# The attention output's transpositions moved from VectorE's 32x32 blocks to TensorE, with quotients out of PSUM

## The chip, the cores and the metric

The kernel runs on one core of a Trainium2 chip. The metric is the device time of one execution in microseconds, the median over runs. The engines are TensorE (PE in the rows; its weight loads are PEld), VectorE (DVE), ScalarE (ACT), GpSimd (POOL) and the DMA queue of SyncE (SP). Each works its own queue of instructions off in order; semaphores connect them.

## What is computed

Two layers over x of 4 x 512 x 128 (batch, tokens, channels). Both begin with attention of 16 heads of 8 channels over a context of 154 keys, on layer-normalized queries; the second is causally masked. Cut to what matters here:

```python
def _L0_xattn_ref(q, k, v, Wq, bq, Wk, bk, Wv, bv, Wo, bo):
    ...
    attn = jax.nn.softmax(jnp.einsum('bhqd,bhkd->bhqk', qh, kh) * scale, axis=-1)
    out = jnp.einsum('bhqk,bhkd->bhqd', attn, vh)
    out = out.transpose(0, 2, 1, 3).reshape(B, Nq, C)
    return out @ Wo.T + bo
...
x = x + jnp.tanh(g_xattn[0]) * _L0_xattn_ref(_layernorm(x, axis=-1), ctx_1024, ...)
x = x + jnp.tanh(g_ffn[0]) * _L0_ffn_ref(_layernorm(x, axis=-1), ...)
x = x + jnp.tanh(g_xattn[1]) * _L1_xattn_ref(_layernorm(x, axis=-1), ctx_1024, ...)
x = x + jnp.tanh(g_ffn[1]) * _L1_ffn_ref(_layernorm(x, axis=-1), ...)
```

The first feed-forward block is quantized with scales taken over whole tensors, so it starts only when the attention of all batches is done. The second is a recurrence of gates over the four batches.

## The kernel before

**Stages and slots.** The program runs, for each layer, a loop over i from -1 to 4, and in each over 20 slots. Stage i makes the 20 score tiles of batch i on TensorE (function `scores`, one per slot, line 985 for whole key tiles, line 991 for the tails of 26 keys); ScalarE takes the exponential of each (`exps`, line 772); TensorE multiplies them with the values (`weigh`, line 1017, six rounds of four tiles: four rounds and two tails). The two tail rounds of batch i-1 run at the start of stage i, in slots 1 and 3. Their results stand in two PSUM banks, `pv[0]` and `pv[1]`, with the sums of the softmax beside the 8 channels of each head. Score tiles go through two PSUM banks (five in the last batch of layer 0), so score t waits for exponential t-2.

**The other work of a stage.** TensorE also makes for batch i+1, in units of up to three heads, the scores from which the row maxima come (`scores_for_top`, line 953; masks line 957), into three banks `top`; VectorE reduces each unit (`take_top`, line 1333). When all are reduced, VectorE splits the maxima (`split_top`, lines 1344 and 1346), TensorE turns them (line 967), ScalarE copies (line 763), and SyncE carries them by DMA into `Q4`. Score 0 of the next stage waits for this DMA. In stage 1 the normalized rows of batch 3 are turned (line 930) and projected to queries (line 936, ScalarE's reads at 744, 751, 755). The turned output of the attention is projected by `project_out` (line 1026, "wo"), VectorE adds the residual (line 1372) and takes the statistics (1293, 1296) for the next norm, POOL its root (628) and, for most batches, the normalized rows (643). One PSUM bank, `misc`, is shared by all these steps in the order of `misc_plan`; each user waits until the one before has been read.

**What sets the order.** It is written out by hand: `PE_PLAN`, `ACT_PLAN` and `DVE_PLAN` are lists of (slot, step, which batch). In a slot each engine does its score tile or exponential and its units of tops first and then the planned steps, in the list's order. In layer 1 the plans also carry the steps of the recurrence ("state", "step"; lines 1037, 1048), in stages 3 and 4. In stage 4 of layer 0, which has no scores, the keys of layer 1 are made (`keys`, line 911 on TensorE, 713 on ScalarE, 1244 on VectorE).

**The output's turning.** In `divide` VectorE transposes each accumulator bank in blocks of 32x32 (line 1353), takes the reciprocals (1356), the products (1359) and transposes back (1366) into `oT`, in slots 3, 3, 5 and 6 of stage i for batch i-1; "wo" follows on TensorE in slot 8 and the residual on VectorE in slot 8.

## Time and profile before

| | us |
|---|---|
| median of 3 runs | 343.34 (343.32 to 343.42) |
| span of the profiled execution | 341.2 |
| TensorE busy in it | 279.0 |
| VectorE busy | 252.5 |
| ScalarE busy | 192.6 |
| POOL busy | 136.7 |

The span is the time from the first to the last instruction of one profiled execution; the device time has some 2 us around it. A profile does not give this execution's own device time, and the runs agree within 0.1 us, so the median stands for it. Times of the rows are us from the span's start unless marked ns; a matmul's duration includes the time until its result is there, so successive matmuls overlap. The attention of layer 0 lies in the first 130 us, the quantized block up to some 205, layer 1 behind it.

### The profile page before, as it was taken

How to read it: one execution, taken by the hardware profiler on the slowest of the kernel's cores; microseconds unless marked ns; L12 is line 12 of the kernel's file. 1: busy time of each engine (PE TensorE's matmuls, PEld its weight loads, DVE VectorE, ACT ScalarE, POOL GpSimd, SP SyncE). 2: the span in 40 equal slices, each digit the busy share in tenths (PEclk: the TensorE clock that was granted, in tenths of full speed). 3: DMA queues.
4: the chain of work that ended last, by engine and by line, in shares of the span. 5: the costliest groups of instructions: out<-in, count | busy, mean ns of one | idle time of the engine just before them, and what ended most of it. 6: DMA issues, size and time to landing. Idle time of an engine off the chain costs nothing. (4 is left out here: it accounts for less than half of the span.)

```text
span 341.2 us, 4468 instructions
## 1 busy us (share of the span) xinstructions
PE 279.0 (82%) x1424; PEld 160.7 (47%) x1424; DVE 252.5 (74%) x538; ACT 192.6 (56%) x303; POOL 136.7 (40%) x274
## 2 busy tenths in 40 slices
PE   0889899899989779985007888899998998999994
PEld 0558544455434345331005776664654654444462
DVE  5699875877996388889989977986596693441834
ACT  1673367556476746779589632446656446665232
POOL 6669893750050411870002059921386207131100
PEclk9999999999999999997556999999999999999998
DMA  7930100010000000000000002220001000000004
GB/s 204 336 146 3 69 32 10 27 73 10 1 8 3 0 0 2 1 0 0 1 0 0 2 0 92 94 100 2 10 25 76 8 0 10 1 0 3 0 1 123
DMA packets 9687, 12.55 MB, mean 37 GB/s; under 512 B 896, under 2 KB 5376, under 8 KB 9664
## 3 DMA queue, kind: packets, MB, share of 16 engines
q1 hardware_dynamic: 9232, 11.80, 9.7%
q10 hardware_dynamic: 432, 0.47, 0.7%
q8 instruction: 11, 0.18, 0.2%
q14 instruction: 12, 0.10, 0.1%
HBM read 4.27 MB, written 1.05 MB: 16 GB/s over the span
## 5 line engine op out<-in xcount | busy, mean ns | idle before, releaser
L1333 DVE TENSOR_REDUCE sb_nm<-ps_top 128x3 f32<-128x462 f32 (+2 forms) x168 | 96.0, 626 | 26.6 <-PE ps_top L953 13.9
L772 ACT ACTIVATE sb_pr<-ps_score 128x512 f32<-128x512 f32 (+1 forms) x148 | 82.3, 583 | 58.8 <-PE ps_score L985 49.2
L953 PE MATMUL ps_top<-sb_Kd,sb_Q 128*128 128x462 f32 (+3 forms) x240 | 69.7, 349 | 4.7 <-DVE sb_nm L1333 2.4
L985 PE MATMUL ps_score<-sb_Q,sb_Kd 128*128 128x512 f32 x119 | 54.4, 467 | 1.3 <-ACT sb_pr L772 1.0
L953 PEld LDWEIGHTS ps_top<-sb_Kd,sb_Q 128*128 128x128 f32 x240 | 42.6, 188 | 18.1 <-DVE sb_nm L1333 11.9
L626 POOL TENSOR_SCALAR sb_var<-sb_mv 128x4 f32<-128x4 f32 x16 | 4.7, 291 | 83.3 <-DVE sb_mv L1296 82.9
L985 PEld LDWEIGHTS ps_score<-sb_Q,sb_Kd 128*128 128x128 f32 x119 | 22.2, 188 | 31.6 <-ACT sb_pr L772 23.4
L1017 PE MATMUL ps_pv<-sb_pr,sb_V 128*32 128x512 f32 x256 | 34.1, 605 | 0.0
L620 POOL TENSOR_SCALAR_AFFINE_SELECT sb_pr<-sb_pr 128x512 f32<-128x512 f32 x16 | 10.6, 661 | 46.4 <-ACT sb_pr L772 46.4
L1353 DVE STREAM_TRANSPOSE sb_oq<-ps_pv 128x512 f32<-128x512 f32 x16 | 10.8, 700 | 12.4 <-PE ps_pv L1017 12.3
L643 POOL TENSOR_SCALAR sb_xn<-sb_xr,sb_nmean,sb_rstd 128x128 f32<-128x128 f32 x44 | 19.3, 453 | 1.2
L628 POOL TENSOR_TENSOR sb_rstd<-sb_var,sb_half 128x4 f32<-128x4 f32 x16 | 17.7, 1106 | 1.3
L521 POOL CAST sb_Kd<-sb_K 32x616 fp32r<-32x616 f32 x20 | 14.1, 703 | 8.5 <-DVE sb_K L1244 7.4
L1017 PE MATMUL ps_pv<-sb_pr,sb_VT 128*32 128x512 f32 (+1 forms) x128 | 14.9, 550 | 0.9 <-ACT sb_pr L772 0.9
L1102 PE MATMUL ps_top<-sb_wfT 128*128 128x256 f32 x30 | 9.5, 472 | 7.2 <-DVE sb_amax L1470 6.4
L991 PE MATMUL ps_score<-sb_Q,sb_KT 128*128 128x384 f32 (+1 forms) x29 | 12.9, 454 | 2.7 <-ACT sb_pr L772 2.7
L1293 DVE BATCH_NORM_STATS2 sb_stat<-sb_xr 128x6 f32<-128x128 f32 x64 | 13.9, 280 | 1.4 <-DMA sb_xr<-x 1.2
L497 POOL MEMSET sb_Q<- 128x2048 f32 x1 | 1.8, 1804 | 32.6 <-DVE sb_amax L1470 32.6
L930 PE MATMUL ps_misc<-sb_consts,sb_xn 128*128 128x128 f32 x64 | 10.4, 287 | 5.1 <-POOL sb_xn L643 2.3
L1195 PE MATMUL ps_top<-sb_front,sb_wfT 128*128 128x512 f32 x22 | 12.1, 682 | 2.7 <-ACT sb_uf L830 2.2
L1084 PE MATMUL ps_misc<-sb_consts,sb_amx 128*128 128x128 f32 x8 | 2.5, 400 | 14.2 <-DVE sb_amx L1403 14.2
L604 POOL TENSOR_TENSOR sb_xg<-sb_xr,sb_bog 128x128 f32<-128x128 f32 x32 | 13.6, 457 | 0.1
(180 smaller groups left out, 556.5 us busy)
## 6 DMA issues: line engine op xcount, KB each, us to landing
sb_Q<-sb_qh SPq DMA_DIRECT2D x16, 256.0 KB, 2.3
sb_Q<-sb_ql SPq DMA_DIRECT2D x8, 256.0 KB, 3.3
sb_xr<-x SPq DMA_DIRECT2D x4, 256.0 KB, 7.7
out<-sb_xr SPq DMA_DIRECT2D x4, 256.0 KB, 2.5
sb_wsb<-w SPq DMA_DIRECT2D x1, 704.0 KB, 9.0
sb_wf<-wffn SPq DMA_DIRECT2D x1, 576.0 KB, 8.6
sb_wkr<-wkr SPq DMA_DIRECT2D x2, 256.0 KB, 7.1
sb_Q<-sb_nmT SPq DMA_DIRECT2D x16, 32.0 KB
```

The source lines that it names most:

```text
L521: ins = pool.tensor_copy(Kd[n % 3][q, :, j, :], K4[q, :, b, :])
L604: ins = pool.tensor_tensor(xg[:, n % 2, t, :], xr[:, TT * b + t, :], bog[:, layer, :], ALU.add)
L628: pool.tensor_tensor(rstd[:, k % 4, :], var[:, k % 4, :], half[:, :], ALU.pow).then_inc(rstd_r, 1)
L643: ins = pool.tensor_scalar(xn[:, kind == "post", t, :], xr[:, TT * b + t, :], nmean[:, k % 4, t:t + 1], rstd[:, k % 4, t:t + 1], ALU.add, ...
L772: act.activation(pr[:, k % PRING, q0:T], score_bank(B * layer + b, t)[:, q0:T], ACT.Exp, scale=SCALE).then_inc(exp_r, 1)
L953: ins = pe.matmul(cols[:, c0:c1, :], Q4[n % 3][:, g, P * qt:P * qt + P], Kd[n % 3][:, g, j:j + c1 - c0, 0:keys], start=True, stop=not mask ...
L985: ins = pe.matmul(ps[:, :], Kd[n % 3][:, g, j, 0:P], Q4[n % 3][:, g, :], start=True, stop=True, skip_group_check=True)
L991: ins = pe.matmul(ps[:, q0:T], KT[:, b, t - H, :], Q4[n % 3][:, t - H, q0:T], start=True, stop=(layer == 0), skip_group_check=True)
L1017: ins = pe.matmul(acc[32 * g:32 * g + 32, q0:T], lhs, pr[:, (TILES * n + t) % PRING, q0:T], start=(r in (0, 2)), stop=(r >= 4), skip_group ...
L1195: pe.matmul(fbank[t % FRING][:, :], wfT[:, 3 * (t // 12) + m, :], xq[:, c, :], start=True, stop=True).then_inc(fmm, 1)
L1293: ins = dve.bn_stats(stat6[:, k % 4, t, :], xr[:, TT * b + t, :])
L1333: dve.tensor_reduce(nm[:, :, :].rearrange("p t h -> p (t h)")[:, f0:f0 + heads], top[k % MRING][:, 0:keys * heads].rearrange("p (h k) -> p ...
```

## The change

ScalarE copies each accumulator bank out of PSUM into a new tile `pvs` ("take0", "take1", line 774 of the changed kernel), TensorE turns the four 128x128 blocks of it back into the same bank ("turn0", "turn1", line 1043), VectorE takes reciprocals and products directly out of PSUM into `oc` (lines 1390 and 1395, one pair per bank), TensorE turns `oc` into `misc` ("out", line 1050), and ScalarE copies that to `oT` (line 778). The turns stand in slots 3, 5 and 7, the copies in slots 2, 4 and 8, the quotients in slots 5 and 6. "wo" and the residual move from slot 8 to 9, the statistics behind them from 9 to 10. One of ScalarE's key copies in stage 4 moves from slot 7 to 10.

```diff
-PE_PLAN = [(1, "tail0", -1), (3, "tail1", -1), (4, "pre", 2), (7, "pre", 3), (6, "q", 2), (10, "q", 3), (7, "round0", 0), (8, "wo", -1),
+PE_PLAN = [(1, "tail0", -1), (3, "tail1", -1), (3, "turn0", -1), (4, "pre", 2), (5, "turn1", -1), (7, "pre", 3), (6, "q", 2),
+           (10, "q", 3), (7, "out", -1), (7, "round0", 0), (9, "wo", -1),
...
-ACT_PLAN = [(5, "pre", 2), (6, "q", 2), (14, "top", 1), (7, "pre", 3), (10, "q", 3), (16, "post", -1),
+ACT_PLAN = [(2, "take0", -1), (4, "take1", -1), (8, "out", -1), (5, "pre", 2), (6, "q", 2), (14, "top", 1), (7, "pre", 3), (10, "q", 3), (16, "post", -1),
...
-DVE_PLAN = [(0, "stat pre", 2), (3, "pre", 2), (3, "div0", -1), (3, "div1", -1), (5, "div2", -1), (6, "div3", -1),
-            (7, "q", 2), (8, "wo", -1), (9, "stat post", -1), (13, "top", 1), (14, "post", -1), (16, "amax", -1),
+DVE_PLAN = [(0, "stat pre", 2), (3, "pre", 2), (5, "div0", -1), (6, "div1", -1),
+            (7, "q", 2), (9, "wo", -1), (10, "stat post", -1), (13, "top", 1), (14, "post", -1), (16, "amax", -1),
...
-NEXT_KEYS_ACT = {4: (0, 1, 2, 3), 7: (4, 5), 10: (6, 7)}
+NEXT_KEYS_ACT = {4: (0, 1, 2, 3), 7: (4,), 10: (5, 6, 7)}
...
-            oq = sb_here("oq", [P, 2, T // 32, 2, 16])
-            oc = sb_here("oc", [P, T // 32, 2, 2, D])
+            pvs = sb_here("pvs", [P, 2, T])
+            oc = sb_here("oc", [P, TT, G, 2, 2, D])
...
+            def take_out(layer, b, part):
+                n = B * layer + b
+                act.wait_ge(pv_r, ROUNDS * n + 5 + part)
+                if n > 0:
+                    act.wait_ge(pvT_r, 2 * n - 1 + part)
+                act.activation(pvs[:, part, :], pv[part][:, :], ACT.Copy).then_inc(pvs_r, 1)
+
+            def copy_out(layer, b):
+                act.wait_ge(misc_full, use["out", layer, b] + 1)
+                act.activation(oT[:, :], misc[:, :], ACT.Copy).then_inc(oT_r, 1)
...
+            def turn_out(layer, b, part):
+                pe.wait_ge(pvs_r, 2 * (B * layer + b) + part + 1)
+                for t in range(TT):
+                    ins = pe.transpose(pv[part][:, P * t:P * t + P], pvs[:, part, P * t:P * t + P], ident[:, :])
+                ins.then_inc(pvT_r, 1)
+
+            def turn_back(layer, b):
+                pe.wait_ge(pvx, 2 * (B * layer + b) + 2)
+                fill_misc(pe, ("out", layer, b))
+                for t in range(TT):
+                    ins = pe.transpose(misc[:, P * t:P * t + P], oc[:, t, :, :, :, :].rearrange("p g a e d -> p (g a e d)"),
+                                       ident[:, :])
+                ins.then_inc(misc_full, 1)
...
-                if part < 2:
-                    dve.wait_ge(pv_r, ROUNDS * n + 5 + part)
-                    dve.transpose(oq[:, part, :, :, :].rearrange("p k e r -> p (k e r)"), pv[part][:, :]).then_inc(pvx, 1)
...
-                    dve.transpose(oT[:, :], oc[:, :, :, :, :].rearrange("p k a e d -> p (k a e d)")).then_inc(oT_r, 1)
+                dve.wait_ge(pvT_r, 2 * n + part + 1)
+                src = pv[part][:, :].rearrange("p (t g e r) -> p t g e r", t=TT, g=G, e=2)
+                dve.reciprocal(orc[:, part, :, :, :], src[:, :, :, :, D]).then_inc(orc_r, 1)
+                dve.wait_ge(orc_r, 2 * n + part + 1)
+                if part == 0 and n > 0:
+                    dve.wait_ge(misc_full, use["out", (n - 1) // B, (n - 1) % B] + 1)
+                dst = oc[:, :, :, part, :, :].rearrange("p t g e d -> p (t g) e d")
+                dve.tensor_tensor(dst, src[:, :, :, :, 0:D].rearrange("p t g e d -> p (t g) e d"),
+                                  orc[:, part, :, :, :].rearrange("p t g e -> p (t g) e").unsqueeze(3)
+                                  .to_broadcast([P, TT * G, 2, D]), ALU.mult).then_inc(pvx, 1)
```

TensorE in layer 0's stage 2, from slot 6 to round 0, before and then after (in the changed kernel line 1004 is `scores`, 972 the tops, 1036 the rounds):

```order
L985 MATMUL ps_score<-sb_Q,sb_Kd 128x512 [waits exp_r]
L953 MATMUL ps_top<-sb_Kd,sb_Q 128x462 [waits top_red]
L985 MATMUL ps_score<-sb_Q,sb_Kd 128x512 [waits exp_r]
L953 MATMUL ps_top<-sb_Kd,sb_Q 128x154 [waits top_red]
L953 MATMUL ps_top<-sb_Kd,sb_Q 128x308
L953 MATMUL ps_top<-sb_Kd,sb_Q 128x308 [waits top_red]
L953 MATMUL ps_top<-sb_Kd,sb_Q 128x154
L1017 MATMUL ps_pv<-sb_pr,sb_V 32x512 [waits exp_r,pvx]
```

```order
L1043 MATMUL ps_pv<-sb_consts,sb_pvs 128x128 [waits pvs_r]
L1043 MATMUL ps_pv<-sb_consts,sb_pvs 128x128 x3
L1004 MATMUL ps_score<-sb_Q,sb_Kd 128x512 [waits exp_r]
L972 MATMUL ps_top<-sb_Kd,sb_Q 128x462 [waits top_red]
L1004 MATMUL ps_score<-sb_Q,sb_Kd 128x512 [waits exp_r]
L972 MATMUL ps_top<-sb_Kd,sb_Q 128x154 [waits top_red]
L972 MATMUL ps_top<-sb_Kd,sb_Q 128x308
L972 MATMUL ps_top<-sb_Kd,sb_Q 128x308 [waits top_red]
L972 MATMUL ps_top<-sb_Kd,sb_Q 128x154
L1050 MATMUL ps_misc<-sb_consts,sb_oc 128x128 [waits xnT_r,pvx]
L1050 MATMUL ps_misc<-sb_consts,sb_oc 128x128 x3
L1036 MATMUL ps_pv<-sb_pr,sb_V 32x512 [waits exp_r,pvx]
```

Turn 1 stands ahead of slot 6, and the turn back, which waits for both of VectorE's products (`pvx`) and for the bank's last reader, ahead of round 0.

TensorE in layer 0's stage 3, where no units of tops stand between the scores, from tail 1 to round 0, before and then after:

```order
L1017 MATMUL ps_pv<-sb_pr,sb_VT 32x512 x3
L985 MATMUL ps_top<-sb_Q,sb_Kd 128x512 [waits top_red]
L985 MATMUL ps_score<-sb_Q,sb_Kd 128x512 [waits exp_r] x2
L985 MATMUL ps_top<-sb_Q,sb_Kd 128x512 [waits exp_r]
L1017 MATMUL ps_pv<-sb_pr,sb_V 32x512 [waits exp_r,pvx]
```

```order
L1036 MATMUL ps_pv<-sb_pr,sb_VT 32x512 x3
L1043 MATMUL ps_pv<-sb_consts,sb_pvs 128x128 [waits pvs_r]
L1043 MATMUL ps_pv<-sb_consts,sb_pvs 128x128 x3
L1004 MATMUL ps_top<-sb_Q,sb_Kd 128x512 [waits top_red]
L1004 MATMUL ps_score<-sb_Q,sb_Kd 128x512 [waits exp_r]
L1043 MATMUL ps_pv<-sb_consts,sb_pvs 128x128 [waits pvs_r]
L1043 MATMUL ps_pv<-sb_consts,sb_pvs 128x128 x3
L1004 MATMUL ps_score<-sb_Q,sb_Kd 128x512 [waits exp_r]
L1004 MATMUL ps_top<-sb_Q,sb_Kd 128x512 [waits exp_r]
L1050 MATMUL ps_misc<-sb_consts,sb_oc 128x128 [waits xnT_r,pvx]
L1050 MATMUL ps_misc<-sb_consts,sb_oc 128x128 x3
L1036 MATMUL ps_pv<-sb_pr,sb_V 32x512 [waits exp_r,pvx]
```

Between tail 1 and round 0 stand four scores, as before, and now three groups of turns, each with a wait for another engine.

VectorE in layer 0's stage 2, before and then after:

```order
L1353 STREAM_TRANSPOSE sb_oq<-ps_pv 128x512 [waits pv_r] x2
L1333 TENSOR_REDUCE sb_nm<-ps_top 128x3 [waits top_r] x3
L1356 RECIPROCAL sb_orc<-sb_oq 128x64 [waits pvx]
L1359 TENSOR_TENSOR sb_oc<-sb_oq,sb_orc 128x16x16 [waits chain]
L1359 TENSOR_TENSOR sb_oc<-sb_oq,sb_orc 128x16x16
L1333 TENSOR_REDUCE sb_nm<-ps_top 128x3 [waits top_r]
L1366 STREAM_TRANSPOSE sb_oT<-sb_oc 128x512 [waits misc_full,oc_r]
```

```order
L1370 TENSOR_REDUCE sb_nm<-ps_top 128x3 [waits top_r] x12
L1390 RECIPROCAL sb_orc<-ps_pv 128x32 [waits pvT_r]
L1395 TENSOR_TENSOR sb_oc<-ps_pv,sb_orc 128x16x16 [waits misc_full,orc_r]
L1370 TENSOR_REDUCE sb_nm<-ps_top 128x3 [waits top_r]
L1390 RECIPROCAL sb_orc<-ps_pv 128x32 [waits pvT_r]
L1395 TENSOR_TENSOR sb_oc<-ps_pv,sb_orc 128x16x16 [waits orc_r]
```

The transpositions are gone; each pair of quotients now stands behind the units of slot 5 or 6.

## Rows read from the trace of the kernel before

**Rows 1.** The page, busy us, share of the span, instructions, by engine.
```profile
PE 279.0 (82%) x1424; PEld 160.7 (47%) x1424; DVE 252.5 (74%) x538; ACT 192.6 (56%) x303; POOL 136.7 (40%) x274
```

**Rows 2.** Groups by line: names, shapes, count | busy us, mean ns | idle before, releasers.
```profile
L1353 DVE STREAM_TRANSPOSE sb_oq<-ps_pv 128x512 f32<-128x512 f32 x16 | 10.8, 700 | 12.4 <-PE ps_pv L1017 12.3
...
L1356 DVE RECIPROCAL sb_orc<-sb_oq 128x64 f32<-128x64 f32 x8 | 4.4, 544 | 0.1
...
L1359 DVE TENSOR_TENSOR sb_oc<-sb_oq,sb_orc 128x256 f32<-128x256 f32 x16 | 7.0, 480 | 0.3
...
L1366 DVE STREAM_TRANSPOSE sb_oT<-sb_oc 128x512 f32<-128x512 f32 x8 | 5.7, 706 | 0.1
...
L1254 DVE RECIPROCAL sb_wabs<-sb_wabs 128x36 f32<-128x36 f32 x1 | 0.4, 379 | 0.0
...
L1333 DVE TENSOR_REDUCE sb_nm<-ps_top 128x3 f32<-128x462 f32 (+2 forms) x168 | 96.0, 626 | 26.6 <-PE ps_top L953 13.9 <-PE ps_top L957 12.4
...
L930 PE MATMUL ps_misc<-sb_consts,sb_xn 128*128 128x128 f32 x64 | 10.4, 287 | 5.1 <-POOL sb_xn L643 2.3 <-DVE sb_ql L1324 1.7 <-DVE sb_xn L1308 0.6
...
L744 ACT ACTIVATE sb_xnT<-ps_misc 128x512 f32<-128x512 f32 x8 | 4.8, 596 | 7.2 <-PE ps_misc L930 6.9
...
L772 ACT ACTIVATE sb_pr<-ps_score 128x512 f32<-128x512 f32 (+1 forms) x148 | 82.3, 583 | 58.8 <-PE ps_score L985 49.2 <-PE ps_score L994 5.2 <-PE ps_score L991 2.4
```

**Rows 3.** Timeline of TensorE, layer 0's stage 2: start us, us, instructions, idle before.
```profile
82.85 1.06 PE L1017 MATMUL ps_pv<-sb_pr,sb_VT 128*32 128x512 f32 x8
...
86.34 1.02 PE L953 MATMUL ps_top<-sb_Kd,sb_Q 128*128 128x154 f32 x4
87.29 1.07 PE L1017 MATMUL ps_pv<-sb_pr,sb_V 128*32 128x512 f32 x8
...
89.30 1.16 PE L1026 MATMUL ps_misc<-sb_wsb,sb_oT 128*128 128x128 f32 x8
...
90.74 0.39 PE L985 MATMUL ps_score<-sb_Q,sb_Kd 128*128 128x512 f32 x1
...
100.95 0.47 PE L985 MATMUL ps_score<-sb_Q,sb_Kd 128*128 128x512 f32 x1 [0.54 <-ACT sb_pr L772]
```

**Rows 4.** Timeline of VectorE, the same stage.
```profile
82.26 1.73 DVE L1333 TENSOR_REDUCE sb_nm<-ps_top 128x3 f32<-128x462 f32 x3 [0.61 <-PE ps_top L953]
83.91 1.30 DVE L1353 STREAM_TRANSPOSE sb_oq<-ps_pv 128x512 f32<-128x512 f32 x2
...
90.78 0.73 DVE L1372 SCALAR_TENSOR_TENSOR sb_xr<-ps_misc,sb_tg,sb_xg 128x512 f32<-128x512 f32 x1
...
95.68 0.31 DVE L1344 CAST sb_nms<-sb_nm 128x64 fp32r<-128x64 f32 x1
```

**Rows 5.** Timeline of TensorE, layer 0's stages 3 and 4.
```profile
103.42 1.07 PE L1017 MATMUL ps_pv<-sb_pr,sb_VT 128*32 128x512 f32 x8
...
107.45 1.16 PE L1026 MATMUL ps_misc<-sb_wsb,sb_oT 128*128 128x128 f32 x8 [0.41 <-DVE sb_oT L1366]
...
108.68 0.40 PE L985 MATMUL ps_score<-sb_Q,sb_Kd 128*128 128x512 f32 x1
...
123.51 1.16 PE L1026 MATMUL ps_misc<-sb_wsb,sb_oT 128*128 128x128 f32 x8 [0.18 <-DVE sb_oT L1366]
```

**Rows 6.** Timeline of VectorE, layer 0's stage 4, up to the feed-forward part.
```profile
124.71 0.75 DVE L1372 SCALAR_TENSOR_TENSOR sb_xr<-ps_misc,sb_tg,sb_xg 128x512 f32<-128x512 f32 x1 [0.38 <-PE ps_misc L1026]
...
130.14 0.16 DVE L1403 TENSOR_REDUCE sb_amx<-sb_amax 128x1 f32<-128x4 f32 x1
```

**Rows 7.** Timeline of ScalarE, layer 1's stage 1.
```profile
253.93 0.68 ACT L755 ACTIVATE sb_qf<-ps_misc,sb_cols 128x512 f32<-128x512 f32 x1
```

**Rows 8.** Timeline of TensorE, layer 1's stage 4.
```profile
319.72 1.16 PE L1026 MATMUL ps_misc<-sb_wsb,sb_oT 128*128 128x128 f32 x8 [0.51 <-DVE sb_oT L1366]
...
324.83 2.84 PE L1037 MATMUL ps_top<-sb_cst,sb_wsb 128*128 128x512 f32 x6
```

29 lines of the change are left out of this document (14 added, 15 removed).

## The prediction

> **What bounds the kernel now.** I first read the busy shares of the page: TensorE is busy for 82% of the span and VectorE for 74% [rows 1], so neither is full over the whole program. Next I read the groups by line, for the price of each operation that the change touches [rows 2]. Then the timeline, engine by engine, of the stages in which a batch's attention output is made. Stage i of a layer is the stretch in which TensorE makes the scores of batch i while the output of batch i-1 is finished; each layer has four stages (1 to 4) that contain such an output. In the stage of layer 0 that runs from 79.32 to 100.95, TensorE goes from step to step with short gaps [rows 3], while VectorE is nearly full with reductions of the score tops, and it is VectorE's split of the last tops, at 95.68 [rows 4], that leads to the DMA on which the next stage's first score, at 100.95 [rows 3], hangs. So a middle stage is a chain that alternates between TensorE and VectorE, in fixed order. What counts is less how busy an engine is than how long one queue stands still for another.
>
> **VectorE's part.** Before, an output costs two block transpositions of 700 ns, a reciprocal of 544, two products of 480 and a transposition of 706 [rows 2]; in the queue that is some 3.2 us (successive ones overlap a little). After, it is two reciprocals of 32 columns and two products. A reciprocal takes 379 ns for 36 columns and 544 for 64 [rows 2], so I estimate 0.40 for 32 columns out of PSUM. A product is 0.40 to 0.48. With the semaphores between them, half an output takes 0.85, and the whole 1.7. VectorE gains 1.5 us an output, 12 us over eight.
>
> **TensorE's part.** It gets three groups of four transpositions of 128x128. Such groups exist already (line 930, 64 of 287 ns each, [rows 2]). These are pipelined: in the timeline a group is followed by the next matmul after 0.41 to 0.5 us. Three groups are 1.3 us an output, 10.5 us over eight. The bounds are 3 x 0.37 and 12 x 0.287 (nothing overlapped), 1.1 and 3.4 us; I take 1.3, since the same instruction stands in the same queue. The Trainium skill, "TensorE: Matmul & The Clock Gate", Part 4: PE-mode transpose, gives about 275 ns for one transposition in a kernel; by it as issue time the twelve would be 3.3 us an output and the forecast some 16 us higher. This trace agrees with it as a duration and not as a spacing.
>
> **ScalarE's part.** Three copies of 128x512 are added, each like the copy of line 744, 596 ns [rows 2], or 0.5 in a row of its kind. It is far from full, so its work costs nothing by itself; but its copies now stand in the chain, each behind an exponential of 583 [rows 2].
>
> **Where the new waits lie.** I work out the stage of layer 0 at 79.32 in full; times are those of the trace. The last tail round starts at 82.85 and lasts 1.06 [rows 3]. The first copy is ready by then, so turn 0 runs at once, to 84.3. Score 4 leaves at 84.3 and is there at 84.8; its exponential lasts to 85.4, the copy of the second accumulator, which is queued behind it, to 85.95. TensorE is ready for turn 1 at 85.55 and waits 0.4. It then does scores 6 and 7 with three units of tops, and is at the turn back by 87.7 (two units take 1.02 in the row at 86.34, [rows 3]). On VectorE the transpositions at 83.91 [rows 4] are gone, but nothing else is there to be done: unit 4 comes only at 85.1 (a unit is one reduction of line 1333, 626 ns [rows 2]; three in a run took 1.73, [rows 4], so 0.55 each). Then units 5 to 86.75, the first quotients to 87.6, unit 6 to 88.15, the second quotients to 89.0. The turn back therefore waits 1.35 on VectorE, and behind it in TensorE's queue stand round 0 and all further scores. Round 0 starts at 89.5, where it was 87.29 [rows 3]. Score 8 is there at 91.0, its exponential ends at 91.65, ScalarE's copy of the turned output, queued behind it, at 92.15. The projection starts at 92.2 instead of 89.30 and score 10 at 93.1 instead of 90.74 [rows 3]. VectorE's residual goes from 90.78 to 93.35 [rows 4]. From the residual to the split of the tops VectorE took 4.9, without a gap [rows 4]; one unit of 0.55 fewer lies in between now, and it waits 0.1 for the tops of slot 10. The split comes at 97.85 instead of 95.68, and the next stage follows it: **+2.2 us**. So VectorE's gain of 1.5 is not lost; it falls into a stretch in which VectorE then waits for TensorE.
>
> **The other stages, the same way.**
> - Layer 0, stage 1: turn 0 hides in TensorE's wait for the normalized rows; the turn back also waits until ScalarE has read the last projection's bank. +2.0.
> - Layer 0, stage 3 has no units of tops between the scores. Tail 1 starts at 103.42 [rows 5]; turn 1 waits for exponential 4 and a copy until 106.5 (1.3 idle), the turn back for VectorE until 108.1 (0.6), the projection for exponential 8 and a copy until 111.25 (1.1). It was at 107.45, and the next score, at 108.68 [rows 5], comes at 112.2. **+3.5**; the later waits for the residual move along.
> - Layer 0, stage 4 has no scores. Turn 1 stands behind five key matmuls (to 124.2), the quotients end at 125.3, the turn back at 125.95. ScalarE's fifth key copy, in front of its copy of the output, needs VectorE's first new key, which is behind the quotients: the copy ends at 126.95, the projection starts at 127.0 instead of 123.51 [rows 5]. From the residual (124.71) to the maximum that opens the feed-forward part (130.14) there is no slack [rows 6]. **+3.4**.
> - Layer 1, stage 1: the turn back needs the shared bank "misc", which ScalarE reads up to 254.6 (copy at 253.93, [rows 7]); the projection of the queries in front of it shifts by 0.7, so the turn back comes at 255.3, round 0 at 255.8. Carried on as above: +2.4.
> - Layer 1, stage 2: waits of 0.4 and 1.4 as in the full case; +2.0.
> - Layer 1, stage 3: the recurrence's matmuls stand between the turns and cover most waits. Three groups and 0.3 of waits: +1.6.
> - Layer 1, stage 4: the projection moves from 319.72 [rows 8] to 322.35, behind the gates' matmuls. Residual, statistics and the update of the state follow one another on VectorE (3.4 us), so the state's next matmul is at 326.95 instead of 324.83 [rows 8]. +2.1.
>
> The sum is 2.0 + 2.2 + 3.5 + 3.4 + 2.4 + 2.0 + 1.6 + 2.1 = **19.2 us**. The feed-forward part between the layers has none of this and only shifts. The profiled execution has a span of 341.2; its time lies 2.1 above it if it equals the median of 343.34. 343.3 + 19.2 = **362.5 us**. Each term hangs on two or three waits that I place to some 0.2, so a term is good to half a microsecond or so; the errors mostly have one sign, since one duration (a copy and its semaphore, half the quotients) is in all of them. Its own range is 356 to 369.
>
> **Rivals.**
> 1. *Only the added work counts.* If copies and quotients are ready in time (durations shorter than I take, or VectorE running close behind TensorE), TensorE pays 10.5 us, and gets back what it waited for VectorE and POOL around these places, about 2: 343.3 + 8.5 = 352. For it speaks that TensorE is the busiest engine; against it the fixed order in which the second quotients stand behind units that TensorE has only just delivered.
> 2. *The relieved VectorE is the bound (faster).* In the four middle stages (1 and 2 of each layer) the split of the tops ends VectorE's chain. If its queue were never empty, each would be 1.5 earlier and the transpositions would fill TensorE's gaps: 343.3 - 6 = 337. It decides when TensorE runs at least three units ahead, so that the missing transpositions are filled with reductions at once. Against it: even now VectorE's queue runs empty, 0.61 us before the tops at 82.26 [rows 4].
> 3. *Twelve transpositions cost their durations.* 3.4 instead of 1.3 an output, partly in place of waits: 362.5 + 10 = 373.
> 4. *No effect*, if gain and cost meet: 343.
>
> I give the forecast 0.74, rival 1 0.13, rival 2 0.06, rival 3 0.05, rival 4 0.02. The range of 8 in 10 takes in rival 1 and most of the forecast's own: 352 to 368. About 0.2% is what a measurement of this kernel tells from no change. Faster 0.06, within 0.2% 0.02, slower 0.92.
>
> **What the changed profile would show.** Right: TensorE's turn back idle for about 1 us on VectorE's products in most stages; the projection idle on ScalarE's copy, in layer 0's stage 3 above all; the first matmul after a group of turns 0.4 to 0.5 after it; the tops' split about 2 later within the stages 1 and 2; stages 3 and 4 of layer 0 longer by some 7 together; VectorE's busy time down by 12 and TensorE's up by 10 to 20. Wrong: turn backs without a wait (then rival 1), or splits earlier than before within their stage (rival 2). If half the quotients took 0.6 instead of 0.85, every middle stage would lose half a microsecond less, and 360 would be the sum.

## The result, and the profile after

The changed kernel takes **362.78 us** (median of 4 runs, 362.45 to 365.68) against 343.37 for the kernel before on the same chip (343.32 to 343.42): 1.058 times as long, with a 95% interval of 1.055 to 1.061. The forecast was 362.5. The profiled execution of the changed kernel is its longest, 365.68 with a span of 363.7; the other three lie at 362.45 to 363.03. Where its 3 us more come from is seen below, in the granted clock. Two executions of the experiments took far longer than the others of their kernel (1434.44 us in experiment 10, 470.04 in experiment 12) and are left out of every time below.

The page of the changed kernel, busy us and share of the span, answers to [rows 1]:

```profile
PE 292.3 (80%) x1520; PEld 173.0 (48%) x1520; DVE 239.0 (66%) x522; ACT 204.5 (56%) x327; POOL 137.4 (38%) x274
```

TensorE has 13.3 us more and ScalarE 11.9, VectorE 13.5 less. The busy time went where it was meant to go, and all three have a smaller share of the span or the same: what grew is the time in which they stand still. (Of TensorE's 13.3 some 2.8 are the lower clock that is shown below, not work.)

The groups by line of the changed kernel answer to [rows 2] (columns as there). In it the numbers of the lines are larger: scores 1004, tops 972, rounds 1036, projection 1059, reductions of the tops 1370, residual 1403. New are ScalarE's copies (774, 778), the turns (1043), the turn back (1050), the reciprocals (1390) and the products (1395).

```profile
L1370 DVE TENSOR_REDUCE sb_nm<-ps_top 128x3 f32<-128x462 f32 (+2 forms) x168 | 96.9, 629 | 39.5 <-PE ps_top L972 24.8 <-PE ps_top L976 14.3
...
L1395 DVE TENSOR_TENSOR sb_oc<-ps_pv,sb_orc 128x256 f32<-128x256 f32 x16 | 6.8, 425 | 0.6
...
L1390 DVE RECIPROCAL sb_orc<-ps_pv 128x32 f32<-128x32 f32 x16 | 5.6, 353 | 22.1 <-PE ps_pv L1043 22.1
...
L774 ACT ACTIVATE sb_pvs<-ps_pv 128x512 f32<-128x512 f32 x16 | 9.5, 593 | 1.6 <-PE ps_pv L1036 1.4
...
L1043 PE MATMUL ps_pv<-sb_consts,sb_pvs 128*128 128x128 f32 x64 | 10.2, 282 | 1.7 <-ACT sb_pvs L774 1.6
```

In [rows 2] VectorE stood still for 26.6 us ahead of its reductions of the tops and for 12.4 ahead of its first transpositions, 39.0 in all. Now it is 39.5 ahead of the reductions alone, and 22.1 more ahead of the reciprocals. So VectorE's 13.5 us less of work did not shorten the kernel: at these two places alone it stands still 22.6 us longer, in a span that is 22.5 longer.

Who waits on TensorE is clearest in the waits of its weight loads in the changed kernel (line, releaser: us in total, times, longest). A weight load comes ahead of each matmul, so the wait shows there first:

```profile
PEld ps_pv L1043 <- ACT sb_pvs L774: 6.5, 8, 1.4
PEld ps_misc L1050 <- DVE sb_oc L1395: 6.2, 6, 1.7
PEld ps_misc L1059 <- ACT sb_oT L778: 5.9, 6, 1.4
```

These are the three links: the turn and the turn back are new, and the projection now waits for ScalarE where it waited for VectorE. The stage that the prediction worked out, layer 0's stage 2, on TensorE in the changed kernel (start, us, instructions, idle before), answers to [rows 3]:

```profile
85.13 1.06 PE L1036 MATMUL ps_pv<-sb_pr,sb_VT 128*32 128x512 f32 x8
86.13 0.66 PE L1043 MATMUL ps_pv<-sb_consts,sb_pvs 128*128 128x128 f32 x4
86.54 0.48 PE L1004 MATMUL ps_score<-sb_Q,sb_Kd 128*128 128x512 f32 x1
...
88.19 0.66 PE L1043 MATMUL ps_pv<-sb_consts,sb_pvs 128*128 128x128 f32 x4 [0.22 <-ACT sb_pvs L774]
...
91.09 0.66 PE L1050 MATMUL ps_misc<-sb_consts,sb_oc 128*128 128x128 f32 x4 [1.09 <-DVE sb_oc L1395]
91.68 1.06 PE L1036 MATMUL ps_pv<-sb_pr,sb_V 128*32 128x512 f32 x8
...
94.44 1.13 PE L1059 MATMUL ps_misc<-sb_wsb,sb_oT 128*128 128x128 f32 x8 [0.62 <-ACT sb_oT L778]
```

The stage begins 2.28 later than before (this tail round at 85.13, in [rows 3] at 82.85). In it turn 1 waits 0.22 (forecast 0.4), the turn back 1.09 (1.35), the projection 0.62 (a wait that the forecast had at about the same size). A group of four turns lasts 0.66, but the next matmul starts 0.41 after the group's start (86.13 to 86.54).

The table sets the profiled executions side by side (the lines below the second are kernels of the experiments, by their numbers; that of 12 is left out, see there), in us more or less than the same stretch of the kernel before. Each stretch runs from the first tail round of a stage (rounds out of sb_VT) to that of the next; the last of layer 0 ends at the global maximum's matmul (130.54 before, 142.21 after), the last but one column at the projection of the last output (319.72 [rows 8], 341.31 after), the last at the end of the span.

```
                            layer 0, stages 1 to 4    ffn  layer 1, stages 1 to 4     end
forecast                     +2.0  +2.2  +3.5  +3.4   0.0  +2.4  +2.0  +1.6  +2.1      
changed kernel               +2.2  +2.1  +3.9  +3.4  +0.1  +4.1  +1.9  +1.4  +2.4  +0.9
1: round 0 first             +1.2  +0.9  +3.2  +4.8  -0.1  +1.3  +0.7  +1.4  +2.4  -0.5
2: copies first              +1.3  +1.2  +1.6  +3.4   0.0  +2.0  +1.3  +1.5  +2.4  +1.1
3: both orders changed       +0.5  +0.1  +1.4  +4.5  -0.1  +0.8  +0.1  +1.4  +2.4  -0.5
4: turns added to before     +1.1  +0.4  +0.4  +1.3   0.0  +0.8  +0.5  +1.3  +1.4   0.0
5: VectorE's relief only      0.0  -0.6  -0.7  -0.4   0.0  -0.1  -0.8   0.0  -0.7  -0.1
6: no first copies           +2.2  +2.1  +2.8  +4.8  -0.1  +2.5  +1.8  +1.2  +2.3  -0.6
7: a quarter of the turns    +1.8  +1.4  +3.0  +2.6  +0.1  +2.9  +1.2  +0.4  +1.5  +1.1
8: hybrid                    +0.5  +0.2   0.0   0.0   0.0  +0.8  +0.1   0.0   0.0   0.0
9: earlier quotients         +0.5  +0.3   0.0   0.0   0.0  +0.8   0.0   0.0   0.0   0.0
10: later projection         -0.1  +0.1   0.0   0.0   0.0  -0.3  -0.3  -0.1  +1.0  +1.1
11: turn ahead of keys       +0.5  +0.2  +1.4  +1.9   0.0  +0.8  +0.1  +1.4  +2.4  -0.6
```

In the table ffn is the feed-forward part with layer 1's first stage, in which no output is made. The first two lines agree within half a microsecond but for layer 1's stage 1 and the end. Both are the clock. The windows of the changed kernel (columns: window, its length, busy us with count of TensorE, its weight loads, VectorE, ScalarE and GpSimd, the **granted clock**, DMA share, GB/s):

```profile
262.00:266.00 4.00, 3.12 (x16) 1.85 (x14) 3.70 (x8) 2.67 (x6) 3.07 (x5) 1.00 0.00 0
266.00:270.00 4.00, 3.07 (x13) 1.10 (x14) 0.00 (x0) 0.79 (x2) 1.86 (x2) 0.61 0.47 177
...
345.80:350.00 4.20, 4.17 (x7) 1.85 (x8) 1.12 (x4) 0.00 (x0) 0.86 (x1) 0.64 0.01 4
```

```profile
266.93 1.08 PE L1050 MATMUL ps_misc<-sb_consts,sb_oc 128*128 128x128 f32 x4 [1.45 <-ACT sb_qf L759]
267.95 1.94 PE L1036 MATMUL ps_pv<-sb_pr,sb_V 128*32 128x512 f32 x8
...
345.83 4.31 PE L1070 MATMUL ps_top<-sb_cst,sb_wsb 128*128 128x512 f32 x6 [1.26 <-DVE sb_cst L1428]
```

The second fence is TensorE's timeline at these two places. TensorE had stood still for 1.45 and for 1.26; a round then takes 1.94 (1.06 elsewhere) and six state matmuls 4.31, which took 2.84 in [rows 8]. The clock is at its lower level (1.2 GHz) for parts of both stretches. Together that is 0.9 + 0.4 + 1.5 = 2.8 us (the second term is the turn back, 1.08 for 0.66), about what this execution takes over the other three. That those lack the two falls fits their times but is not shown, since each kernel has one profile.

### The profile page after: what moved, and what is told of

Same layout as the page of the kernel before. It is cut to its first block and busy times, and to the rows that moved or that the text cites. A ratio compares the mean times of both kernels' runs of the same rounds, so it can differ in the third digit from the quotient of the medians.

```text
span 363.7 us, 4690 instructions
## 1 busy us (share of the span) xinstructions
PE 292.3 (80%) x1520; PEld 173.0 (48%) x1520; DVE 239.0 (66%) x522; ACT 204.5 (56%) x327; POOL 137.4 (38%) x274
## 5 line engine op out<-in xcount | busy, mean ns | idle before, releaser
L1370 DVE TENSOR_REDUCE sb_nm<-ps_top 128x3 f32<-128x462 f32 (+2 forms) x168 | 96.9, 629 | 39.5 <-PE ps_top L972 24.8
L972 PE MATMUL ps_top<-sb_Kd,sb_Q 128*128 128x462 f32 (+3 forms) x240 | 67.5, 344 | 2.9 <-DVE sb_nm L1370 1.0
L1004 PE MATMUL ps_score<-sb_Q,sb_Kd 128*128 128x512 f32 x119 | 55.9, 475 | 1.5 <-ACT sb_pr L787 1.5
L1036 PE MATMUL ps_pv<-sb_pr,sb_V 128*32 128x512 f32 x256 | 35.0, 619 | 0.0
L1390 DVE RECIPROCAL sb_orc<-ps_pv 128x32 f32<-128x32 f32 x16 | 5.6, 353 | 22.1 <-PE ps_pv L1043 22.1
L1403 DVE SCALAR_TENSOR_TENSOR sb_xr<-ps_misc,sb_tg,sb_xg 128x512 f32<-128x512 f32 x8 | 6.0, 751 | 18.9 <-PE ps_misc L1059 18.9
L1070 PE MATMUL ps_top<-sb_cst,sb_wsb 128*128 128x512 f32 x24 | 13.6, 667 | 1.3 <-DVE sb_cst L1428 1.3
```

What stands on the lines that cost most here:

```text
L972: ins = pe.matmul(cols[:, c0:c1, :], Q4[n % 3][:, g, P * qt:P * qt + P], Kd[n % 3][:, g, j:j + c1 - c0, 0:keys], start=True, stop=not mask ...
L1004: ins = pe.matmul(ps[:, :], Kd[n % 3][:, g, j, 0:P], Q4[n % 3][:, g, :], start=True, stop=True, skip_group_check=True)
L1036: ins = pe.matmul(acc[32 * g:32 * g + 32, q0:T], lhs, pr[:, (TILES * n + t) % PRING, q0:T], start=(r in (0, 2)), stop=(r >= 4), skip_group ...
L1070: ins = pe.matmul(top[k][:, :], weight((UF, UI, UC)[k]), cst[:, :], start=(b != X_FIRST), stop=(b == X_FIRST), skip_group_check=True)
L1370: dve.tensor_reduce(nm[:, :, :].rearrange("p t h -> p (t h)")[:, f0:f0 + heads], top[k % MRING][:, 0:keys * heads].rearrange("p (h k) -> p ...
```

## The experiments

"+" is over the kernel before on the same chip (343.06 to 343.22). The changed kernel stands at +19.4.

**1. Round 0 ahead of the turn back.**

```
-           (10, "q", 3), (7, "out", -1), (7, "round0", 0), (9, "wo", -1),
+           (10, "q", 3), (7, "round0", 0), (7, "out", -1), (9, "wo", -1),
```

> The changed kernel with one edit: in TensorE's order of slot 7, round 0 of the next batch stands ahead of the turn back, not behind it. Round 0 needs only the first quotients. In the changed kernel's trace the turn back waits for VectorE's second product in most stages (1.09 us in the stage that starts at 81.60, six such waits of 6.2 us in all by the weight loads). Theory A (the time goes into waits of TensorE's queue for a chain of ScalarE and VectorE, as predicted): round 0, 1.0 us, fills these waits, -5 us, about 357.5. Rival B (only the added work counts, the waits are cover for something that is late anyway): no change, 362.5 within 0.7.

Measured: 357.79 (356.72 to 359.17), +14.6, ratio 1.042 (1.039 to 1.045). One line of order brings 5.0 back; the rival of no change is out.

**2. ScalarE's copies ahead of the exponentials.**

```
-ACT_PLAN = [(2, "take0", -1), (4, "take1", -1), (8, "out", -1), (5, "pre", 2), (6, "q", 2), (14, "top", 1), (7, "pre", 3),
+ACT_PLAN = [(2, "take0", -1), (3, "take1", -1), (5, "pre", 2), (6, "q", 2), (14, "top", 1), (7, "pre", 3), (7, "out", -1),
```

> The changed kernel with ScalarE's order changed alone: the copy of the second accumulator stands ahead of exponential 4 and not behind it, and the copy of the turned output ahead of exponential 8. Both exponentials wait for a later matmul anyway. In the changed trace TensorE waits at the projection for this copy (0.62 in the stages 1 and 2 of layer 0, 1.04 and 1.07 in stages 3 and 4, 0.33 in two of layer 1) and at turn 1 for the other (0.22 to 0.94). Theory A: the projection's waits go, 4 us, and of turn 1's, 3 us in all, most comes back at the turn back, since that one waits for VectorE: -4 to -6, about 357.5. Rival B: no change within 0.7.

Measured: 359.15 (357.84 to 359.54), +16.0, ratio 1.045 (1.043 to 1.048): 3.6 back, a little under the expected 4 to 6. The rival is out here too. ScalarE's work is the same; only its place in the queue changed.

**3. Both orders.**

> Both edits in one: round 0 ahead of the turn back, and ScalarE's two copies ahead of exponentials 4 and 8. Theory A: the waits are different ones, so the gains add: -9 to -11, 352 to 353, and what is left over the kernel before, 9 us, is TensorE's added work (24 groups of four transpositions at 0.41). Rival B: 362.5. If the gains overlap (one wait takes the other's place), it is near the better of the two single edits.

Measured: 352.45 (352.17 to 353.73), +9.3, ratio 1.027 (1.025 to 1.029). The gains add up and a bit more (10.3 for 5.0 + 3.6; the runs of the two single edits lie up to 2.4 apart, so the 1.7 more is not clear of them). More than half of the 19.4 us were waits that an order of the queues made. TensorE's timeline of the kernel with both orders, the same stage, which starts here 0.38 later than in [rows 3]:

```profile
83.23 1.07 PE L1036 MATMUL ps_pv<-sb_pr,sb_VT 128*32 128x512 f32 x8
...
85.90 0.60 PE L1043 MATMUL ps_pv<-sb_consts,sb_pvs 128*128 128x128 f32 x4
...
87.92 1.06 PE L1036 MATMUL ps_pv<-sb_pr,sb_V 128*32 128x512 f32 x8 [0.24 <-DVE sb_oc L1395]
89.19 0.66 PE L1050 MATMUL ps_misc<-sb_consts,sb_oc 128*128 128x128 f32 x4 [0.20 <-DVE sb_oc L1395]
...
90.62 1.13 PE L1059 MATMUL ps_misc<-sb_wsb,sb_oT 128*128 128x128 f32 x8
```

Of 1.9 us of waits 0.44 are left, and the stage is 0.1 longer than before the change. The table shows where this kernel's +9.3 lies: in the stages 3 and 4 of both layers. Of the +4.5 in layer 0's stage 4 some 1.5 are a fall of the clock in the profiled execution (shown in experiment 11; the profiles of 1 and 6 have the same one). This execution is, at 353.73, the longest of the four. The recorded account of the rest, that the 9 us left are the added work at 0.41 a group, has the number but not the place: it would be spread over all eight stages, and experiment 4 prices the work lower.

**4. The added work alone.**

```
+            def idle_turns(bank, groups):
+                for t in range(TT * groups):
+                    pe.transpose(bank[:, P * (t % TT):P * (t % TT) + P], ident[:, :], ident[:, :])
...
+                if r in (0, 2) and b > 0:
+                    idle_turns(pv[r // 2], 1)
...
+                idle_turns(misc, 1 if b < B - 1 else 3)
```

> The kernel before, with nothing changed but 12 more transpositions of 128x128 for each output on TensorE, whose results are overwritten: four ahead of the projection's matmuls in their bank, four ahead of rounds 0 and 2 of the next batch in theirs; in the last stage of a layer all twelve ahead of the projection. No wait is added and VectorE's transpositions stay. It prices TensorE's work alone. Theory A (0.41 to 0.44 a group, on the path): 24 groups, +10, 353.5. If a transposition cost its duration of 0.29, +27, 370. If TensorE's gaps hid them, +2 or less.

Measured: 350.18 (350.05 to 350.25), +7.0, ratio 1.020 (1.018 to 1.022). That is less than the +10 of theory A (0.41 a group on the path) and far from +27. 96 transpositions, in about the places of the change, cost 7.0, 0.29 a group, although the same instructions show a duration of 272 to 278 ns each in the groups by line of this kernel:

```profile
L1000 PE MATMUL ps_pv<-sb_consts 128*128 128x128 f32 x48 | 7.2, 272 | 0.0
...
L1000 PE MATMUL ps_misc<-sb_consts 128*128 128x128 f32 x48 | 6.8, 278 | 1.1 <-DVE sb_oT L1373 1.1
```

The table's line for it shows that the price depends on the stage: 0.4 an output in layer 0's stages 2 and 3, up to 1.4 in layer 1's stage 4. The Trainium skill ("TensorE: Matmul & The Clock Gate", Part 4: PE-mode transpose) gives about 275 ns for one in a kernel, measured there in bf16, here it is fp32: as a duration this trace agrees (272 and 278), as a cost on the path the run gives 7.0 / 96 = 0.073 us.

**5. VectorE's relief alone.**

```
-                    dve.transpose(oq[:, part, :, :, :].rearrange("p k e r -> p (k e r)"), pv[part][:, :]).then_inc(pvx, 1)
...
+                    src = pv[part][:, :].rearrange("p (k e r) -> p k e r", e=2, r=16)
+                    link(dve.reciprocal(orc[:, part, :, :], src[:, :, :, D]))
...
+                    dve.tensor_tensor(oT[:, :].rearrange("p (k a e d) -> p k a e d", a=2, e=2, d=D)[:, :, part, :, :],
+                                      src[:, :, :, 0:D], orc[:, part, :, :].unsqueeze(3).to_broadcast([P, T // 32, 2, D]),
+                                      ALU.mult).then_inc(pvx, 1)
...
-                    dve.transpose(oT[:, :], oc[:, :, :, :, :].rearrange("p k a e d -> p (k a e d)")).then_inc(oT_r, 1)
```

> The kernel before with VectorE's three block transpositions of an output left out (so the output is computed from turned-wrong data), its reciprocals and products reading the accumulators in PSUM as in the changed kernel, the products writing the projection's input; nothing is added on TensorE or ScalarE. It prices VectorE's relief alone, about 1.5 to 1.8 us an output. Theory A as recorded in the prediction (the relief falls into stretches where VectorE then waits for TensorE): only stages 3 and 4 gain, 0 to -4, about 341. New theory C, from the kernel with both orders changed, whose stages 1 and 2 are only 0 to 0.8 us longer than before despite 1.3 us more work on TensorE: the relief is worth about 1 us in each of the four middle stages and 1.5 in each last stage, -7 to -9, about 335.5.

Measured: 339.95 (339.80 to 340.18), -3.3, ratio 0.990 (0.988 to 0.992). The number is within theory A's 0 to -4, and theory C's relief of 1 us in each middle stage is not there. But A let only the stages 3 and 4 gain, and by the table the stages 2 give 0.6 and 0.8. The quotients stand here in slot 3, right behind the tail rounds, and not in slots 5 and 6. VectorE's timeline of this kernel, the same stage:

```profile
84.32 0.35 DVE L1354 RECIPROCAL sb_orc<-ps_pv 128x32 f32<-128x32 f32 x1
84.71 0.42 DVE L1357 TENSOR_TENSOR sb_oT<-ps_pv,sb_orc 128x256 f32<-128x256 f32 x1
85.05 0.35 DVE L1354 RECIPROCAL sb_orc<-ps_pv 128x32 f32<-128x32 f32 x1
...
89.71 0.64 DVE L1333 TENSOR_REDUCE sb_nm<-ps_top 128x3 f32<-128x462 f32 x1 [0.57 <-PE ps_top L953]
90.60 0.75 DVE L1369 SCALAR_TENSOR_TENSOR sb_xr<-ps_misc,sb_tg,sb_xg 128x512 f32<-128x512 f32 x1 [0.25 <-PE ps_misc L1026]
...
95.51 0.31 DVE L1344 CAST sb_nms<-sb_nm 128x64 fp32r<-128x64 f32 x1
```

The stage starts 0.4 later than in the kernel before and its split comes at 95.51, where [rows 4] has 95.68: a relief of 1.5 us of work gives some 0.6, and the rest is two new waits for TensorE, 0.57 and 0.25. That is less than half of what the turns cost TensorE. If the two prices add, 7.0 - 3.3 = +3.7 is what the change costs with no new wait. For the four middle stages the sum can be held against a run: 2.8 of work less 1.6 of relief is +1.2, and experiment 3, with few waits left there, has +1.5.

**6. The first copies left out.**

```
-                pe.wait_ge(pvs_r, 2 * (B * layer + b) + part + 1)
...
-                    ins = pe.transpose(pv[part][:, P * t:P * t + P], pvs[:, part, P * t:P * t + P], ident[:, :])
+                    ins = pe.transpose(pv[part][:, P * t:P * t + P], weight(WV).bitcast(F32), ident[:, :])
...
-ACT_PLAN = [(2, "take0", -1), (4, "take1", -1), (8, "out", -1), (5, "pre", 2), (6, "q", 2), (14, "top", 1),
+ACT_PLAN = [(8, "out", -1), (5, "pre", 2), (6, "q", 2), (14, "top", 1),
```

> The changed kernel with ScalarE's two copies of the accumulators left out: the first turns read a constant tile, so they wait for nothing (the output is computed from wrong data); ScalarE's copy of the turned output, the turn back and all orders stay. Theory A: turn 1 no longer waits (8 waits, 6.5 us by the weight loads), but of that the most comes back as a longer wait at the turn back, which hangs on units of tops and quotients on VectorE; gain where nothing covers it, the last stages (1.0 to 2 us each) and stage 3 of layer 0 (0.9): -3 to -5, about 358.5. Rival D (each link of the chain counts in full): two copies of 0.6 and their semaphores an output, -10, 352.

Measured: 361.99 (361.63 to 363.71), +18.8, ratio 1.056 (1.052 to 1.059). Only 0.8 come back, less than either theory gave, and nothing like D's 10. TensorE's timeline of this kernel, the same stage:

```profile
87.52 0.60 PE L1042 MATMUL ps_pv<-sb_consts,sb_wsb 128*128 128x128 f32 x4
...
90.81 0.66 PE L1049 MATMUL ps_misc<-sb_consts,sb_oc 128*128 128x128 f32 x4 [1.52 <-DVE sb_oc L1394]
```

Turn 1 waits no more and the turn back waits 1.52 instead of 1.09: the wait moved one link on, since the quotients stand behind reductions in VectorE's queue. The profiles give what remains: 1.2 in layer 0's stage 3, and 0.2 or less in the stages 1, 2 of layer 0 and 2 to 4 of layer 1. In layer 0's stage 4, where 1 to 2 were expected, the missing link gives nothing: from the first tail round to the projection it takes 8.17 with the copies (126.94 to 135.11) and without (125.47 to 133.64), since turn 1 stands there behind the key matmuls. Behind the projection this profile is 1.4 longer, at a low granted clock. The projections and the maximum's matmuls, of the changed kernel and then of this one, and this one's windows:

```profile
135.11 1.13 PE L1059 MATMUL ps_misc<-sb_wsb,sb_oT 128*128 128x128 f32 x8 [1.07 <-ACT sb_oT L778]
142.21 0.46 PE L1117 MATMUL ps_top<-sb_consts,sb_amx 128*128 128x128 f32 x2 [0.38 <-DVE sb_amx L1434]
```

```profile
133.64 1.13 PE L1058 MATMUL ps_misc<-sb_wsb,sb_oT 128*128 128x128 f32 x8 [1.07 <-ACT sb_oT L778]
142.16 0.39 PE L1116 MATMUL ps_top<-sb_consts,sb_amx 128*128 128x128 f32 x2
```

```profile
135.00:138.00 3.00, 2.46 (x5) 1.17 (x4) 2.93 (x12) 1.21 (x2) 0.95 (x2) 0.50 0.00 0
138.00:141.00 3.00, 3.00 (x14) 2.79 (x13) 2.15 (x7) 0.61 (x2) 0.27 (x1) 0.50 0.02 5
```

Without this fall the run would be at some 360.6 (an estimate, 361.99 less 1.4), still short of the expected -3 to -5. Layer 1's stage 1 shows the opposite: TensorE waits the same 1.45 ahead of the turn back as in the changed kernel, but no fall follows, and the stage is +2.5 where the changed kernel's profile has +4.1.

**7. A quarter of the turns.**

```
-                for t in range(TT):
+                for t in range(1):
```

(in both functions that turn)

> The changed kernel with one transposition in each group instead of four (72 of 96 left out, so the output is computed from partly unturned data); every wait, copy, quotient and order stays. It tells apart whether TensorE's work or the chain's waits make the 19.4 us. The work alone was 7.0 for 24 groups (kernel before with added transpositions). Theory A: the turns are links of the chain, so each is 0.3 shorter and the chain with it: three quarters of 7.0, and the waits stay, -5, 357.5. Rival F (the waits for others absorb TensorE's time): -1 to -2, 361. Rival B (only added work counts): -14, 348.

Measured: 358.07 (357.22 to 359.67), +15.0, ratio 1.044 (1.040 to 1.047): 4.4 to 4.7 less, as theory A has it, and far from the 14 of "only work counts". With three quarters of the work gone, three quarters of the loss are still there. By the table every output is 0.4 to 1.2 shorter than in the changed kernel.

**8. Only the outputs of the middle stages by TensorE.** Both orders as in 3; outputs of batches 0 and 1 by TensorE, 2 and 3 by VectorE's block transpositions in the places of the kernel before, projection and residual included.

```
+BY_PE = [(0, 0), (0, 1), (1, 0), (1, 1)]
...
+            (3, "div0", -1), (3, "div1", -1), (5, "quo0", -1), (5, "div2", -1), (6, "quo1", -1), (6, "div3", -1),
```

> Outputs of batches 0 and 1 (stages 1 and 2 of each layer, those with reductions of the tops) go by TensorE, with round 0 ahead of the turn back and ScalarE's copies ahead of the exponentials; those of batches 2 and 3 (stages 3 and 4) go by VectorE's block transpositions, in the places that the kernel before has. Theory C: in the middle stages VectorE's relief pays for TensorE's work (stages 1 and 2 of the kernel with both orders: +0.4, +0.0, +0.8, +0.1), and the whole cost of that kernel, +9.3, lies in stages 3 and 4: 343.2 + 1.3 = 344.5. Theory A' (cost follows the number of outputs turned by TensorE, half of 9.3): 347.8.

Measured: 344.84 (344.26 to 345.99), +1.6, ratio 1.005 (1.003 to 1.006), where 344.5 were expected from the stages alone. In the table its stages 3 and 4 stand at 0.0 and its stages 1 and 2 where the kernel of experiment 3 has them: in this pair of kernels the stages' costs add.

**9. The hybrid with the first quotients a slot earlier.**

```
-            (5, "quo0", -1), (5, "div2", -1), (6, "quo1", -1)
+            (4, "quo0", -1), (5, "div2", -1), (6, "quo1", -1)
```

> The hybrid, and VectorE's first quotients one slot earlier (slot 4), where its queue stands still for about 1.0 us before the next tops and the first turned accumulator is ready (84.6 against 85.4 in the stage at 79.7). Theory C: VectorE is the end of these stages' chain, 0.5 us less in each of four: 342.5, 0.2% below the kernel before. Rival: TensorE's supply of tops is the bound there, no change from the hybrid.

Measured: 344.83 (344.57 to 345.13), ratio 1.004 (1.003 to 1.006). No change from the hybrid, so theory C is wrong in this point. In layer 0's stage 2 the first quotients start 1.2 earlier (85.88 for 87.06), and the split of the tops comes at 96.21 where the hybrid has 96.16: VectorE then waits for TensorE's tops and projection (0.24 and 0.28), as the rival and experiment 5 have it.

**10. The later projection alone.**

```
-           (10, "q", 3), (7, "round0", 0), (8, "wo", -1),
+           (10, "q", 3), (7, "round0", 0), (9, "wo", -1),
...
-            (7, "q", 2), (8, "wo", -1), (9, "stat post", -1),
+            (7, "q", 2), (9, "wo", -1), (10, "stat post", -1),
```

> The kernel before with only the change's shift of the plan: projection and residual one slot later (9 for 8), the statistics one later (10 for 9). Nothing else. It prices the shift, which was not costed apart. Theory C: the projection then waits no longer for VectorE's last transposition (0.41 and 0.65 in stages 3 and 2), and the residual comes 0.5 to 0.8 later in its stage with other reductions drawn ahead of it: 0 to +2 over eight outputs, 344. Rival E: the shift is what costs, since residual, statistics, POOL and post turn hang on it: +0.8 a stage, +6, 349.

Measured: 344.22 in the median of nine, +1.2, ratio 1.002 (1.000 to 1.004). The runs fall into two groups, four at 342.79 to 343.21, the same as before, and five at 344.22 to 345.18. In the faster group the shift costs nothing, and rival E is out; the profiled execution (345.18) belongs to the second group. Its window at the end, and TensorE there:

```profile
324.00:330.00 6.00, 4.82 (x11) 2.33 (x12) 2.20 (x6) 0.00 (x0) 1.92 (x2) 0.72 0.00 1
```

```profile
325.18 4.50 PE L1037 MATMUL ps_top<-sb_cst,sb_wsb 128*128 128x512 f32 x6 [1.26 <-DVE sb_cst L1397]
```

The later output makes TensorE stand still for 1.26 ahead of the state's matmuls, where it had no wait in [rows 8], and these then take 4.50 for 2.84 at a granted clock of 0.72. The 1.7 more are about what parts the two groups. Whether the faster one lacks this fall can't be seen, as none of it was profiled.

**11. In layer 0's last stage, the turn ahead of the keys** (on top of 3).

```
-NEXT_KEYS_PE = {3: (0, 1, 2, 3, 4), 9: (5, 6, 7)}
+NEXT_KEYS_PE = {3: (0, 1), 5: (2, 3, 4), 9: (5, 6, 7)}
```

> The changed kernel with both orders changed (352.45), and in layer 0's last stage the second turn ahead of three of the five key matmuls that stand before it in TensorE's queue. In that kernel's trace the second accumulator's copy is ready at 123.1, its turn starts at 125.52, behind ten matmuls, and TensorE later waits 0.91 and 0.78 for quotients and copy, after which the granted clock is 0.50 to 135.5. Theory C: the chain starts 2 us earlier, -2 from the order, and up to 2.5 more if the clock stays at 1.00: 348 to 350.5. Rival: keys and statistics on VectorE are the end there, no change, 352.4.

Measured: 351.44 (351.28 to 352.14), +8.4, ratio 1.025 (1.023 to 1.026). That is 1.0 less than with both orders; 2 or more were expected, so this forecast missed by half, though its rival of no change is out. By the profiles the stage is 2.6 shorter (+1.9 for +4.5), in two parts. From the first tail round to the projection it takes 6.76 for 7.88: that is the order, 1.1, as the medians say. From the projection to the maximum's matmul it takes 7.01 for 8.53 (7.03 in the kernel before): in this stretch the profiled execution of experiment 3 has a fall of the clock and this one none. TensorE's timeline of the kernel of 3 at the waits, then a window of that kernel and one of this:

```profile
127.03 0.65 PE L1050 MATMUL ps_misc<-sb_consts,sb_oc 128*128 128x128 f32 x4 [0.91 <-DVE sb_oc L1395]
128.46 1.24 PE L1059 MATMUL ps_misc<-sb_wsb,sb_oT 128*128 128x128 f32 x8 [0.78 <-ACT sb_oT L778]
```

```profile
130.50:133.00 2.50, 1.97 (x5) 0.88 (x4) 2.45 (x11) 1.21 (x2) 1.02 (x2) 0.50 0.00 0
```

```profile
131.00:133.00 2.00, 1.88 (x14) 1.74 (x15) 1.83 (x7) 1.22 (x2) 1.02 (x1) 1.00 0.00 0
```

**12. The waits filled** (on top of 3).

```
+                if (layer, b) == (0, B - 1):
+                    idle_turns(misc, 2)
                 pe.wait_ge(pvx, 2 * (B * layer + b) + 2)
...
+                if (layer, b) == (0, B - 1):
+                    idle_turns(pv[0], 2)
                 pe.wait_ge(oT_r, n + 1)
```

> The changed kernel with both orders changed (352.45), and in layer 0's last stage TensorE's two waits (0.91 for the quotients, 0.78 for ScalarE's copy) filled with eight useless transpositions each, 0.8 us, ahead of the wait. If the fall of the granted clock from 1.00 to 0.50 between 129 and 135.5 follows from TensorE standing still there, it stays at 1.00 and the stage is 2 to 2.5 shorter: 350. If the clock falls anyway: 352.5 to 353, the fillers costing up to 0.3.

Measured: 352.49 in the median of three (352.30 to 352.71), +9.4, ratio 1.027 (1.026 to 1.029); the profiled execution is the one left out, so no trace shows the stage. There is no gain over experiment 3. The run settles less than it was meant to. Its 350 takes the fall's cost off the median 352.45, but three of the four executions of experiment 3 (352.17 to 352.47) are already 1.3 to 1.6 shorter than the profiled one (353.73), about what the fall costs there, so they may not have it. Whether the filled waits keep the clock up stays open.

## Why the forecast came true, point by point

- **The chain of waits is the mechanism.** The three waits stand where they were forecast, with 0.22, 1.09 and 0.62 us in the worked-out stage. "In most stages" is too much for the turn back's wait on VectorE: four of the eight have it (1.09, 0.44, 0.91, 1.30), in the stages 1 it waits for ScalarE's read of the shared bank (0.76, 1.45), as the terms of these stages said, and in layer 1's stages 3 and 4 for nothing. Over all stages TensorE stands still for 11.5 us at the three links, against 1.8 at the projections before. Experiments 1 to 3 take 10.3 of 19.4 us back by order alone, and experiment 7 leaves 15 us with little of the work. What the experiments add to the forecast is the budget: work +7.0 (experiment 4), relief -3.3 (experiment 5), and so, if these add, 15.7 for waits and what they bring along. The links' own 11.5 - 1.8 = 9.7 are seen in the rows; where the other 6 lie was not traced.
- **TensorE's work was mis-sized.** "Three groups are 1.3 us an output, 10.5 us over eight" is right as spacing (0.41 a group in the rows above), but on the path it is 7.0 (experiment 4).
- **VectorE's gain was mis-sized.** The forecast let it go wholly into stretches of waiting. It does so for the larger part; 3.3 of 12 us come through in experiment 5. The two errors partly cancel in rival 1, whose 352 thus came from 8.5 of added work where the runs give 3.7.
- **Half the quotients** were taken at 0.85. Reciprocal and product measure 353 and 425 ns, and in VectorE's timeline of experiment 5 the second half follows the first after 0.73 (84.32 to 85.05), as in the changed kernel the reductions follow the first half after 0.72. Two halves of some 0.13 less are the 0.26 by which the turn back's wait, 1.09, falls short of 1.35. No saving in the stages follows: the hedge (0.6 instead of 0.85, half a microsecond less in every middle stage) would have given a quarter microsecond, and they came out at +2.2, +2.1 and +1.9 for +2.0, +2.2 and +2.0.
- **The stages.** Of the eight terms seven are within 0.5 of the profile; the largest miss among these is layer 0's stage 3, +3.9 for +3.5. Its three waits are shorter than placed (0.94, 0.44 and 1.04 for 1.3, 0.6 and 1.1), so the work between them was placed too short. That the total meets the median within 0.3, closer than its terms meet the profile, is luck: their misses partly cancel. The last term ends at the state's matmul, as the prediction defined it: 345.83 - 324.83 is 21.0, of which 19.15 had come together by the stage's first tail round (333.22 - 314.07), so +1.9 for +2.1. Layer 1's stage 1 was +4.1 for +2.4, the clock's share in it below.
- **What was not thought of is the clock.** The prediction took all matmuls at the durations of [rows 3, 8]. In the profiles of the changed kernels the granted clock falls behind new waits, at places where it was at 1.00 before, at different ones in different kernels' profiles. In the profiled execution of the changed kernel that is about 3 us, half of it in layer 1's stage 1 and half behind the last term; where layer 1's stage 1 shows no fall (experiment 6) it is +2.5. The median, 362.78, is 2.9 below this execution and so, it seems, free of most of it.
- **Rivals.** Rival 1 (only the added work counts) is refuted for this kernel by the result, 362.78 for 352, and by experiments 1, 2 and 7. With both orders the time is 352.45, near its 352, but by another sum: +3.7 of work and relief, and the waits left in stages 3 and 4. Rival 2 (a relieved VectorE makes it faster) is out by the result, and experiments 5 and 9 say why: relief brought 3.3 with nothing added, and an earlier quotient brought nothing. Rival 4 (no effect) is out by the result. Rival 3 (transpositions cost their durations) would have shown +27 in experiment 4 and gave +7.0.
- **Where it is lost even with the best order.** In the middle stages relief and work nearly cancel (+0.1 to +0.8 in experiment 3). In stages 3 and 4 the relief is worth as much (0.0 to 0.7), but three groups of turns and three copies replace a chain of 3.2 us on one engine by one over three. The Trainium skill ("VectorE: DVE Perf Modes", Rules for kernel authors) gives a full 128x128 transposition to TensorE, and calls VectorE's the fastest for 32x32 blocks. The kernel before needed blocks only, and the runs side with the second line: 3.3 us for VectorE's way, 7.0 for TensorE's before any wait. That it is this longer chain which makes these stages dear is argued; of its orders there, only those of experiments 1, 2 and 11 were tried. No version that turns outputs on TensorE and computes the whole result is faster than the kernel before; the hybrid is the nearest, 0.5% slower.
